# A gated graph network in groups of four tiles, with the next aggregation and s_hi moved ahead of z

## The chip, the cores and the metric

One core of one Trainium2 chip. The metric is the device time of an execution in microseconds (us). The kernel before has a median of 377.11 us over three runs (376.7 to 378.42).

## The reference, cut to what matters

Sixty-four graphs of 128 nodes with 128 features. A layer norm and a relu give the first state, five layers each aggregate over neighbours and update the state with a GRU cell, and the masked state is added to x.

```python
def _gru_cell(m, h, w_ih, w_hh, b_ih, b_hh):
    gi = m @ w_ih.T + b_ih
    gh = h @ w_hh.T + b_hh
    i_r, i_z, i_n = jnp.split(gi, 3, axis=-1)
    h_r, h_z, h_n = jnp.split(gh, 3, axis=-1)
    r = jax.nn.sigmoid(i_r + h_r)
    z = jax.nn.sigmoid(i_z + h_z)
    n = jnp.tanh(i_n + r * h_n)
    return (1.0 - z) * n + z * h
...
A = (adj != 0).astype(x.dtype)
h = jnp.maximum(_layernorm(x, axis=-1), 0.0)
for l in range(5):
    m = jnp.einsum('bnd,de->bne', h, weight[l])
    agg = jnp.einsum('bij,bid->bjd', A, m)
    h = _gru_cell(agg, h, w_ih, w_hh, b_ih, b_hh)
return x + h * mask[..., None]
```

## The kernel before, in words

**Tiles and units.** A tile is four graphs, so there are 16 tiles of 128 partitions x 512 columns. The state is kept with features on partitions (h, float32), with its fp16 high and low halves in hp. A unit is one layer of one tile, and there are 80 of them. `GROUPS = (4, 6, 6)` sets their order (line 45): layer 0 of all tiles of a group, then layer 1 of all, and so on. A tile's next layer thus comes four units later in the first group and six later in the others.

**One unit on TensorE** (lines 386 to 407). The layer's weight and w_ih are folded into one matrix V of that layer by `fold`, so that S, the aggregated state, is multiplied by V, and h by w_hh. Every float32 product is three fp16 matmuls (lines 273 to 275 for h, and for S). In order: the h products of r, z and n into ps_r, ps_z, ps_hn; the S products of r and z into the same banks; `aggregate(K + 1)`, eight small matmuls that sum over neighbours for the next unit into ps_s (lines 344 to 347); and the S product of n into ps_in. S products wait for s_lo of their unit, the h products of r, z and n for r, z and rhn of the unit before.

**The rest of a unit.** ScalarE (ACT): r = sigmoid(ps_r), z = sigmoid(ps_z), s_hi of the next unit (the fp16 part of ps_s), h_hi of the previous unit's state, and n = tanh. VectorE (DVE): rhn (ps_hn times r), the n input (ps_in + rhn), s_lo of the next unit, then (z - 1) times n and the new h. GpSimd (POOL): zh (z times h), then h_lo of the previous unit's state (line 783). Every engine works through its queue in the order that the code writes (`for K in range(N)` in each block), whatever is ready.

**The way back.** The aggregation needs the state with nodes on partitions. SyncE (SP) issues a DMA transpose nat<-hp (line 221) once h_lo is done, and `aggregate` waits for its landing (line 341).

**Preparing a tile** (`prep`, lines 53 to 61). While earlier tiles are in work, each tile from 4 on passes through nine stages, one per unit: 0 loads of adjacency and of an x, and moments on DVE; 1 their aggregate and minus_mean on DVE, 1/std on POOL; 2 the adjacency on POOL (line 766); 3 and 4 the two halves of the layer norm on ACT (line 417); 5 nat_hi on ACT and nat_lo on POOL; 6 the DMA transpose hp<-nat (line 209) and the float32 state. Tiles below `HALVES` (10) get that state from four float32 PE transposes (line 356) and a relu on ACT (line 437). Tiles from 10 on get it by splitting each float32 into two 16-bit halves on ACT (`split`, line 444), a DMA transpose of the halves (line 215), and a joining copy on DVE in stage 8 (`join`, line 648). Tiles are 3 units apart up to tile 9, and 5 apart after.

**Finishing a tile.** `ends` (line 60) says in which unit a tile's mask product (line 790) and its sum with x (line 794) run, both on POOL in one unit; SP stores the result an iteration later, and `load_ends` fetches x and the mask six units ahead. Unit 78 has its mask product on DVE.

**Folding.** `folding(K)` (line 187) puts the folds of layers 1 to 4 at the ends of units 2, 6, 10 and 14; ACT and DVE make v_hi and v_lo of them there.

Of the kernel before, what the change touches and what calls it, by code (L numbers as in the profile page):

```python
# [5 lines left out]
ALU = mybir.AluOpType  # L6
# [8 lines left out]
TG = 4  # L15
# [3 lines left out]
EPS = 1e-05  # L19
GROUPS = (4, 6, 6)  # L20
RING = 10
# [4 lines left out]
DIRECT = 1  # L26
HALVES = 10
FETCH = 6
FINISH = 5
STAGES = 9  # L30
EXPONENT = 0x7F800000
# [5 lines left out]
def gnn_kernel(nc, x, xT, adj, mask_row, fold_lhs, w_ihT, w_hhT, bias_ih, bias_hh, ident, out):  # L37
# [8 lines left out]
    N = len(units)  # L46
    at = {u: K for K, u in enumerate(units)}


# [4 lines left out]
    for t in reversed(range(FIRST, TILES)):  # L54
        gap = 3 if t < starts[1] + GROUPS[1] else 5
        prep[t] = min(at[t, 0] - STAGES, prep[t + 1] - gap if t + 1 < TILES else N)
    ends = {}
    for t in range(TILES - 1):
        soon = at[t, LAST] + 1
        ends[t] = soon if t >= starts[-1] or not t else max(soon, ends[t - 1] + 3)  # L60
    tile_at_stage = [{prep[t] + s: t for t in prep} for s in range(STAGES)]
    ending = {ends[t]: t for t in ends}
    fetching = {ends[t] - FETCH: [t] for t in ends}
    fetching[N - FINISH - FETCH].append(TILES - 1)

# [4 lines left out]
    with ExitStack() as ctx:  # L70
# [86 lines left out]
        nat_hi_init, nat_lo_init = sem("nat_hi_init"), sem("nat_lo_init")  # L157
        split_done = sem("split_done")
        h_hi_init, h_lo_init, h_init = sem("h_hi_init"), sem("h_lo_init"), sem("h_init")
# [34 lines left out]
        def _(sp):  # L194
# [16 lines left out]
            def transpose_halves(t):  # L211
                sp.wait_ge(split_done, t - HALVES + 1)
                if t - HALVES >= 2:
                    sp.wait_ge(h_init, t - 1)
                sp.dma_start_transpose(halves_t[:, t % 2], halves[:, t % 2].rearrange("p b c -> p (b c)")).then_inc(
                    halves_loaded[t % 2], 16)
# [35 lines left out]
            for K in range(1, N + 2):  # L252
# [6 lines left out]
                if K in tile_at_stage[6]:  # L259
                    transpose_first(tile_at_stage[6][K])  # L260
                    if tile_at_stage[6][K] >= HALVES:
                        transpose_halves(tile_at_stage[6][K])
                if K - 1 in ending:
                    store(ending[K - 1])
                for t in fetching.get(K, ()):
# [5 lines left out]
        def _(pe):  # L271
# [114 lines left out]
            for K in range(N):  # L386
                if K:
                    h_products(K)
                else:
                    first_h_products()  # L390
                if K == N - 1:
                    break
                pe.wait_ge(s_lo_done, K + 1)
                if K < L * FIRST and K % FIRST == 0:
                    pe.wait_ge(v_lo_done, units[K][1] + 1)
                s_product(K, 0, ps_r).then_inc(r_mm, 1)
                s_product(K, 1, ps_z).then_inc(z_mm, 1)
                if K + 1 < FIRST:
                    transpose_first(K + 1)
                if tile_at_stage[5].get(K, HALVES) < HALVES:  # L400
                    transpose_first(tile_at_stage[5][K])
                aggregate(K + 1)
                if K >= 2:
                    pe.wait_ge(h_done, K - 1)
                s_product(K, 2, ps_in[K % 2]).then_inc(in_mm, 1)
                if folding(K):
                    fold(folding(K))

        @block.scalar
        def _(act):  # L410
            def layernorm(t, half):
                act.wait_ge(shift_done, t + 1)
                if t >= LN:
                    act.wait_ge(nat_lo_init, t - LN + 1)
                    act.wait_ge(t_mm, min(t - LN + 1, HALVES))
                for q in (2 * half, 2 * half + 1):
# [14 lines left out]
            def transposed(t):  # L431
                act.wait_ge(t_mm, t + 1)
                if t < DIRECT:
                    act.wait_ge(h_lo_init, t + 1)
                if t >= RING:
                    act.wait_ge(masked, t - RING + 1)
                nc.scalar.activation(h[:, t % RING], ps_t[:], ACT.Relu).then_inc(h_init, 1)

            def split(t):

                act.wait_ge(h0_done, 2 * t + 2)
                if t - HALVES >= 2:
                    act.wait_ge(halves_loaded[t % 2], 16 * ((t - HALVES) // 2))
                nc.scalar.copy(halves[:, t % 2], h0[:, t % LN].bitcast(U16).rearrange("p (c b) -> p b c", b=2)).then_inc(
                    split_done, 1)
# [72 lines left out]
            for K in range(N):  # L518
                if K < N - 1:
# [3 lines left out]
                    if K == 1:  # L523
                        gate_n(0)
                    gate_z(K)
                    s_high(K + 1)
                else:
# [22 lines left out]
                if K in tile_at_stage[5]:  # L550
                    natural_high(tile_at_stage[5][K])
                if K in tile_at_stage[6] and tile_at_stage[6][K] < HALVES:
                    transposed(tile_at_stage[6][K])
                if K in tile_at_stage[6] and tile_at_stage[6][K] >= HALVES:
                    split(tile_at_stage[6][K])
# [3 lines left out]
        def _(dve):  # L559
# [47 lines left out]
            def new_state(K):  # L607
# [6 lines left out]
                dve.wait_ge(zn_done, K + 1)  # L614
                out_ap = h[:, t % RING] if K < N - 2 else ps_in[K % 2][:]
                nc.vector.tensor_tensor(out_ap, zh[:, K % 2], ps_in[K % 2][:], ALU.subtract).then_inc(h_done, 1)  # L616
# [26 lines left out]

            def join(t):
                dve.wait_ge(halves_loaded[t % 2], 16 * ((t - HALVES) // 2 + 1))
                if t >= RING:
                    dve.wait_ge(masked, t - RING + 1)
                nc.vector.tensor_copy(h[:, t % RING].bitcast(U16).rearrange("p (c b) -> p b c", b=2),
                               halves_t[:, t % 2].rearrange("p (b g) c -> p b (g c)", b=2)).then_inc(h_init, 1)

# [66 lines left out]
            for K in range(N):  # L717
# [10 lines left out]
                if K in tile_at_stage[1]:  # L728
                    aggregate(tile_at_stage[1][K])
                    opposite_mean(tile_at_stage[1][K])  # L730
                if tile_at_stage[8].get(K, 0) >= HALVES:
                    join(tile_at_stage[8][K])
                if K == 1:
# [3 lines left out]
                elif K:  # L737
                    masked_open(K)
                    last_result(K)
                if K == N - 2:  # L740
                    masked_state(K)
# [4 lines left out]
        def _(pool):  # L746
# [33 lines left out]
            def state_low(K):  # L780
                t = units[K][0]
                pool.wait_ge(h_hi_done, inner[K])
                nc.gpsimd.tensor_tensor(h_lo(t), h[:, t % RING], h_hi(t), ALU.subtract).then_inc(h_lo_done, 1)  # L783

            def final(t):
                f = t % FRING
                if t < TILES - 2:
                    pool.wait_ge(ends_loaded[f], 32 * (t // FRING + 1))
                    pool.wait_ge(h_done, at[t, LAST] + 1)
                    nc.gpsimd.tensor_tensor(mask_in[:, f], mask_in[:, f], h[:, t % RING], ALU.mult).then_inc(masked, 1)  # L790
                    pool.wait_ge(masked, t + 1)
                else:
                    pool.wait_ge(last_masked, 1)
                nc.gpsimd.tensor_tensor(x_out[:, f], x_out[:, f], mask_in[:, f], ALU.add).then_inc(out_done, 1)
# [27 lines left out]
            for K in range(N):  # L822
# [14 lines left out]
                if K == N - FINISH:  # L837
                    masked_last_h()
                if K in ending and K < N - 1:
                    final(ending[K])  # L840

# [35 lines left out]
```

## Time and profile before

| | before |
|---|---|
| median of 3 runs, us | 377.11 |
| the profiled execution, us | 377.65 |
| its span, first to last instruction, us | 375.9 |
| granted TensorE clock, share of full | 0.996 |
| busy share PE / DVE / ACT / POOL | 97 / 83 / 79 / 73 % |
| DMA queue q1, share of 16 engines' span | 51.7 % |

The span is one profiled execution; the time of the same execution is 1.75 us longer. A matmul's shown duration overlaps the next one's, so the start of one and the start of the next tell the pace, not the duration. In the prediction, a unit is counted from the start of its S product of r, "S of r" for short, and offsets are from there.

### The profile page before, as it was taken

How to read it: one execution, taken by the hardware profiler on the slowest of the kernel's cores; microseconds unless marked ns; L12 is line 12 of the kernel's file. 1: busy time of each engine (PE TensorE's matmuls, PEld its weight loads, DVE VectorE, ACT ScalarE, POOL GpSimd, SP SyncE). 2: the span in 40 equal slices, each digit the busy share in tenths (PEclk: the TensorE clock that was granted, in tenths of full speed). 3: DMA queues.
4: the chain of work that ended last, by engine and by line, in shares of the span. 5: the costliest groups of instructions: out<-in, count | busy, mean ns of one | idle time of the engine just before them, and what ended most of it. 6: DMA issues, size and time to landing. Idle time of an engine off the chain costs nothing.

```text
span 375.9 us, 6545 instructions
## 1 busy us (share of the span) xinstructions
PE 363.5 (97%) x2152; PEld 184.0 (49%) x2152; DVE 310.2 (83%) x572; ACT 297.6 (79%) x495; POOL 275.7 (73%) x258
## 2 busy tenths in 40 slices
PE   7899999999999999999999999999999999999992
PEld 3454555555555544445444545544455545555441
DVE  4879888888878788798989898888878787777775
ACT  5988898998878888798888887687677776677662
POOL 3759779788778979587695876867877655555796
PEclk9999999999999999999999999999999999999998
DMA  8536535747744556745364774327734423287422
GB/s 259 189 58 140 114 74 123 175 95 180 169 111 111 86 94 121 150 87 114 83 115 112 146 192 82 88 58 161 134 70 102 97 56 58 56 228 184 95 84 84
DMA packets 102176, 44.46 MB, mean 118 GB/s; under 512 B 91392, under 2 KB 91776, under 8 KB 102144
## 3 DMA queue, kind: packets, MB, share of 16 engines
q1 hardware_dynamic: 102000, 43.80, 51.7%
q8 instruction: 17, 0.28, 0.3%
q10 hardware_dynamic: 144, 0.26, 0.2%
q14 instruction: 15, 0.12, 0.1%
HBM read 17.57 MB, written 4.19 MB: 58 GB/s over the span
## 4 chain that ended last, share of the span: by engine, by line
PE 79%; DVE 9%; POOL 5%; DMA 2%; issue 2%; SPq 1%; ACT 1%; DVEq 0%; POOLq 0%
PE ps_r L273 8%; PE ps_z L275 8%; PE ps_z L274 8%; PE ps_z L273 8%; PE ps_r L275 8%; PE ps_r L274 8%; PE ps_s L347 4%; PE ps_s L346 4%; PE ps_in L275 4%; PE ps_in L274 4%; PE ps_in L273 4%; PE ps_hn L273 4%; PE ps_hn L275 4%; PE ps_hn L274 4%; DVE ps_in L605 1%
## 5 line engine op out<-in xcount | busy, mean ns | idle before, releaser
L778 POOL TENSOR_TENSOR zh<-z,h 128x512 f32<-128x512 f32 x80 | 101.8, 1272 | 77.3 <-ACT z L461 77.0
L455 ACT ACTIVATE r<-ps_r,b_sum,unscale 128x512 f32<-128x512 f32 x80 | 62.2, 778 | 46.9 <-PE ps_r L275 46.0
L465 ACT ACTIVATE ps_in<-ps_in,b_ih,unscale 128x512 f32<-128x512 f32 x80 | 60.0, 751 | 19.2 <-DVE ps_in L605 17.5
L783 POOL TENSOR_TENSOR hp<-h,hp 128x512 f16<-128x512 f32 x64 | 74.0, 1156 | 1.3 <-ACT hp L471 1.3
L599 DVE SCALAR_TENSOR_TENSOR rhn<-ps_hn,b_hn,r 128x512 f32<-128x512 f32 x80 | 59.9, 749 | 17.1 <-ACT r L455 16.8
L605 DVE TENSOR_TENSOR ps_in<-ps_in,rhn 128x512 f32<-128x512 f32 x80 | 56.0, 699 | 16.0 <-PE ps_in L275 13.7
L611 DVE SCALAR_TENSOR_TENSOR ps_in<-z,ps_in 128x512 f32<-128x512 f32 x79 | 54.6, 691 | 11.0 <-ACT ps_in L465 11.0
L461 ACT ACTIVATE z<-ps_z,b_sum,unscale 128x512 f32<-128x512 f32 x80 | 61.6, 770 | 0.7 <-PE ps_z L275 0.7
L616 DVE TENSOR_TENSOR h<-zh,ps_in 128x512 f32<-128x512 f32 x78 | 53.6, 687 | 10.3 <-POOL zh L778 2.1
L593 DVE TENSOR_TENSOR s_lo<-ps_s,s_hi 128x512 f16<-128x512 f32 x80 | 54.4, 680 | 0.4 <-ACT s_hi L449 0.4
L449 ACT CAST s_hi<-ps_s 128x512 f16<-128x512 f32 x80 | 46.6, 582 | 0.5
L346 PE MATMUL ps_s<-a,nat 128*128 128x128 f16 x320 | 44.3, 219 | 0.0
L347 PE MATMUL ps_s<-a,nat 128*128 128x128 f16 x320 | 44.3, 219 | 0.0
L471 ACT CAST hp<-h 128x512 f16<-128x512 f32 x64 | 40.6, 634 | 2.1 <-DVE h L616 2.1
L346 PEld LDWEIGHTS ps_s<-a,nat 128*128 128x128 f16 x320 | 31.3, 98 | 8.8 <-POOL nat L760 0.4
L347 PEld LDWEIGHTS ps_s<-a,nat 128*128 128x128 f16 x320 | 31.3, 98 | 8.2
L273 PE MATMUL ps_r<-s_hi,v_hi 128*128 128x512 f16 x80 | 30.4, 380 | 2.8 <-DVE s_lo L593 2.6
L273 PE MATMUL ps_z<-s_hi,v_hi 128*128 128x512 f16 x80 | 30.3, 379 | 0.0
L274 PE MATMUL ps_r<-s_lo,v_hi 128*128 128x512 f16 x80 | 30.3, 379 | 0.0
L275 PE MATMUL ps_r<-s_hi,v_lo 128*128 128x512 f16 x80 | 30.3, 379 | 0.0
L274 PE MATMUL ps_z<-s_lo,v_hi 128*128 128x512 f16 x80 | 30.3, 379 | 0.0
L275 PE MATMUL ps_z<-s_hi,v_lo 128*128 128x512 f16 x80 | 30.3, 379 | 0.0
(109 smaller groups left out, 741.3 us busy)
## 6 DMA issues: line engine op xcount, KB each, us to landing
x_in<-in_x SPq DMA_DIRECT2D x16, 256.0 KB, 3.7
adj_in<-in_adj SPq DMA_DIRECT2D x16, 256.0 KB, 3.9
x_out<-in_xT SPq DMA_DIRECT2D x16, 256.0 KB, 3.1
mask_in<-in_mask_row SPq DMA_DIRECT2D x16, 256.0 KB, 3.6
out<-x_out SPq DMA_DIRECT2D x15, 256.0 KB, 2.3
nat<-hp SPq DMA_TRANSPOSE x64, 3.1
fold_in<-in_fold_lhs SPq DMA_DIRECT2D x1, 320.0 KB, 3.9
out<-x_out ACTq DMA_DIRECT2D x1, 256.0 KB, 2.6
```

The source lines that it names most:

```text
L273: nc.tensor.matmul(ps[:], w_hi, m_hi, start=start, stop=False)
L274: nc.tensor.matmul(ps[:], w_hi, m_lo, start=False, stop=False)
L275: return nc.tensor.matmul(ps[:], w_lo, m_hi, start=False, stop=stop)
L346: nc.tensor.matmul(block_of(ps_s, q), block_of(nat_hi(t), q), a_q, start=True, stop=False)
L347: last = nc.tensor.matmul(block_of(ps_s, q), block_of(nat_lo(t), q), a_q, start=False, stop=True)
L455: nc.scalar.activation(r[:], ps_r[:], ACT.Sigmoid, bias=b_sum[:, 0:1], scale=unscale[:, 0:1]).then_inc(r_done, 1)
L461: nc.scalar.activation(z[:, K % 2], ps_z[:], ACT.Sigmoid, bias=b_sum[:, 1:2], scale=unscale[:, 0:1]).then_inc(z_done, 1)
L465: nc.scalar.activation(ps_in[K % 2][:], ps_in[K % 2][:], ACT.Tanh, bias=b_ih[:, 2:3], scale=unscale[:, 0:1]).then_inc(n_done, 1)
L599: nc.vector.scalar_tensor_tensor(out=rhn[:], in0=ps_hn[:], scalar=b_hn[:, 0:1], in1=r[:], op0=ALU.add, op1=ALU.mult).then_inc(rhn_done, 1)
L605: nc.vector.tensor_tensor(ps_in[K % 2][:], ps_in[K % 2][:], rhn[:], ALU.add).then_inc(npre_done, 1)
L778: nc.gpsimd.tensor_tensor(zh[:, K % 2], z[:, K % 2], h[:, t % RING], ALU.mult).then_inc(zh_done, 1)
L783: nc.gpsimd.tensor_tensor(h_lo(t), h[:, t % RING], h_hi(t), ALU.subtract).then_inc(h_lo_done, 1)
```

## The change

`GROUPS` becomes (4, 4, 4, 4). All tiles from 4 on take the way over split, DMA transpose and join. The join is cut in two, in stages 8 and 9, so a preparation has ten stages. With the new constants the tiles 4 to 8 start their preparation at units 4, 7, 10, 13 and 18, tile 9 at 23, and the others every five units from there to 53. The mask product and the final sum of a finished tile run in consecutive units on POOL (units 21 and 22 for tile 0, then every five units up to tile 7 at 56 and 57, then every three); the last group's mask products, units 76 to 78, run on DVE, and its states go to PSUM. Layer 1 is folded in unit 0, ahead of TensorE's wait for s_lo. TensorE does the next aggregation between the S products of r and z, and ACT does s_hi of the next unit ahead of z.

```diff
--- before.py
+++ after.py
@@ -17,17 +17,17 @@
-GROUPS = (4, 6, 6)
+GROUPS = (4, 4, 4, 4)
...
-HALVES = 10
 FETCH = 6
-FINISH = 5
-STAGES = 9
+FINISH = 3
+STAGES = 10
+SPREAD = 5
@@ -45,6 +45,7 @@
+    END = at[starts[-1], LAST]
@@ -52,16 +53,27 @@
     for t in reversed(range(FIRST, TILES)):
-        gap = 3 if t < starts[1] + GROUPS[1] else 5
+        gap = 3 if t < starts[1] + GROUPS[1] else SPREAD
         prep[t] = min(at[t, 0] - STAGES, prep[t + 1] - gap if t + 1 < TILES else N)
     ends = {}
     for t in range(TILES - 1):
         soon = at[t, LAST] + 1
-        ends[t] = soon if t >= starts[-1] or not t else max(soon, ends[t - 1] + 3)
+        if t >= starts[-1]:
+            ends[t] = soon
+        elif t and ends[t - 1] > prep[TILES - 1]:
+            ends[t] = max(soon, ends[t - 1] + 3)
+        else:
+            ends[t] = max(soon, ends[t - 1] + SPREAD if t else 0)
+            ends[t] += (prep[TILES - 1] + 3 - ends[t]) % SPREAD
...
+    adds = {t: ends[t] + (ends[t] + 1 not in ending and ends[t] + 2 < N) for t in ends}
+    adding = {adds[t]: t for t in ends if t < TILES - 2}
+    storing = {adds[t] + 1: t for t in ends}
@@ -258,10 +270,9 @@
                 if K in tile_at_stage[6]:
                     transpose_first(tile_at_stage[6][K])
-                    if tile_at_stage[6][K] >= HALVES:
-                        transpose_halves(tile_at_stage[6][K])
-                if K - 1 in ending:
-                    store(ending[K - 1])
+                    transpose_halves(tile_at_stage[6][K])
+                if K in storing:
+                    store(storing[K])
@@ -390,20 +401,20 @@
                 if K == N - 1:
                     break
+                if K == 0:
+                    fold(1)
                 pe.wait_ge(s_lo_done, K + 1)
                 if K < L * FIRST and K % FIRST == 0:
                     pe.wait_ge(v_lo_done, units[K][1] + 1)
                 s_product(K, 0, ps_r).then_inc(r_mm, 1)
-                s_product(K, 1, ps_z).then_inc(z_mm, 1)
                 if K + 1 < FIRST:
                     transpose_first(K + 1)
-                if tile_at_stage[5].get(K, HALVES) < HALVES:
-                    transpose_first(tile_at_stage[5][K])
                 aggregate(K + 1)
+                s_product(K, 1, ps_z).then_inc(z_mm, 1)
                 if K >= 2:
                     pe.wait_ge(h_done, K - 1)
                 s_product(K, 2, ps_in[K % 2]).then_inc(in_mm, 1)
-                if folding(K):
+                if folding(K) > 1:
                     fold(folding(K))
@@ -522,8 +531,8 @@
+                    s_high(K + 1)
                     gate_z(K)
-                    s_high(K + 1)
@@ -549,9 +558,7 @@
-                if K in tile_at_stage[6] and tile_at_stage[6][K] < HALVES:
-                    transposed(tile_at_stage[6][K])
-                if K in tile_at_stage[6] and tile_at_stage[6][K] >= HALVES:
+                if K in tile_at_stage[6]:
                     split(tile_at_stage[6][K])
@@ -612,7 +619,7 @@
-                out_ap = h[:, t % RING] if K < N - 2 else ps_in[K % 2][:]
+                out_ap = h[:, t % RING] if K < END else ps_in[K % 2][:]
@@ -641,12 +648,17 @@
-            def join(t):
-                dve.wait_ge(halves_loaded[t % 2], 16 * ((t - HALVES) // 2 + 1))
+            def join(t, half):
+
+                dve.wait_ge(halves_loaded[t % 2], 16 * ((t - FIRST) // 2 + 1))
                 if t >= RING:
                     dve.wait_ge(masked, t - RING + 1)
-                nc.vector.tensor_copy(h[:, t % RING].bitcast(U16).rearrange("p (c b) -> p b c", b=2),
-                               halves_t[:, t % 2].rearrange("p (b g) c -> p b (g c)", b=2)).then_inc(h_init, 1)
+                two = slice(2 * half, 2 * half + 2)
+                state = h[:, t % RING].rearrange("p (g c) -> p g c", g=TG)[:, two].rearrange("p g c -> p (g c)")
+                joined = nc.vector.tensor_copy(state.bitcast(U16).rearrange("p (c b) -> p b c", b=2),
+                                               halves_t[:, t % 2].rearrange("p (b g) c -> p b g c", b=2)[:, :, two].rearrange(
+                                                   "p b g c -> p b (g c)"))
+                joined.then_inc(h_init if half else half_joined, 1)
@@ -728,8 +740,9 @@
-                if tile_at_stage[8].get(K, 0) >= HALVES:
-                    join(tile_at_stage[8][K])
+                for half in range(2):
+                    if K in tile_at_stage[8 + half]:
+                        join(tile_at_stage[8 + half][K], half)
@@ -737,7 +750,7 @@
-                if K == N - 2:
+                if END <= K < N - 1:
                     masked_state(K)
@@ -782,15 +795,18 @@
+            def masked_result(t):
+                f = t % FRING
+                pool.wait_ge(ends_loaded[f], 32 * (t // FRING + 1))
+                pool.wait_ge(h_done, at[t, LAST] + 1)
+                nc.gpsimd.tensor_tensor(mask_in[:, f], mask_in[:, f], h[:, t % RING], ALU.mult).then_inc(masked, 1)
+
             def final(t):
                 f = t % FRING
-                if t < TILES - 2:
-                    pool.wait_ge(ends_loaded[f], 32 * (t // FRING + 1))
-                    pool.wait_ge(h_done, at[t, LAST] + 1)
-                    nc.gpsimd.tensor_tensor(mask_in[:, f], mask_in[:, f], h[:, t % RING], ALU.mult).then_inc(masked, 1)
+                if t < starts[-1]:
                     pool.wait_ge(masked, t + 1)
                 else:
-                    pool.wait_ge(last_masked, 1)
+                    pool.wait_ge(last_masked, t - starts[-1] + 1)
                 nc.gpsimd.tensor_tensor(x_out[:, f], x_out[:, f], mask_in[:, f], ALU.add).then_inc(out_done, 1)
@@ -836,8 +852,10 @@
-                if K in ending and K < N - 1:
-                    final(ending[K])
+                if K in ending and ending[K] < starts[-1]:
+                    masked_result(ending[K])
+                if K in adding:
+                    final(adding[K])
```

## Rows read from the trace of the kernel before

**Rows 1.** Section 1 of the page: busy us, share of the span, instructions.
```profile
PE 363.5 (97%) x2152; PEld 184.0 (49%) x2152; DVE 310.2 (83%) x572; ACT 297.6 (79%) x495; POOL 275.7 (73%) x258
```
**Rows 2.** Timeline of unit 64: start us, us, engine, line, operation, [idle before it].
```profile
301.86 0.38 PE L273 MATMUL ps_r<-s_hi,v_hi 128*128 128x512 f16 x1
...
302.71 0.78 ACT L455 ACTIVATE r<-ps_r,b_sum,unscale 128x512 f32<-128x512 f32 x1 [1.11 <-PE ps_r L275]
...
303.39 0.77 ACT L461 ACTIVATE z<-ps_z,b_sum,unscale 128x512 f32<-128x512 f32 x1
303.52 0.75 DVE L599 SCALAR_TENSOR_TENSOR rhn<-ps_hn,b_hn,r 128x512 f32<-128x512 f32 x1 [0.40 <-ACT r L455]
...
304.05 0.58 ACT L449 CAST s_hi<-ps_s 128x512 f16<-128x512 f32 x1
304.23 1.27 POOL L778 TENSOR_TENSOR zh<-z,h 128x512 f32<-128x512 f32 x1 [1.95 <-ACT z L461]
...
304.45 0.70 DVE L605 TENSOR_TENSOR ps_in<-ps_in,rhn 128x512 f32<-128x512 f32 x1 [0.18 <-PE ps_in L275]
...
304.51 0.64 ACT L471 CAST hp<-h 128x512 f16<-128x512 f32 x1
...
304.90 0.38 PE L273 MATMUL ps_z<-hp,u_hi 128*128 128x512 f16 x1
305.06 0.68 DVE L593 TENSOR_TENSOR s_lo<-ps_s,s_hi 128x512 f16<-128x512 f32 x1
...
305.97 0.69 DVE L611 SCALAR_TENSOR_TENSOR ps_in<-z,ps_in 128x512 f32<-128x512 f32 x1 [0.23 <-ACT ps_in L465]
...
306.19 0.38 PE L273 MATMUL ps_r<-s_hi,v_hi 128*128 128x512 f16 x1
```
**Rows 3.** Windows view of units 4 to 77: busy us of each engine, clock, DMA.
```profile
34.00:362.50 328.50, 326.69 (x1954) 166.44 (x1955) 276.92 (x479) 264.95 (x433) 245.32 (x219) 1.00 0.53 114
```
**Rows 4.** The chain that ended last, between 34 and 363 us: start us, us, what.
```profile
44.13 0.44 PE ps_t L356 x4
45.66 0.65 PE ps_f L362 x2
...
113.22 0.44 PE ps_t L356 x4
```
**Rows 5.** Groups of instructions: busy us, mean ns of one | idle before.
```profile
L417 ACT ACTIVATE h<-x_in,shift,rstd 128x128 f32<-128x128 f32 x64 | 27.4, 484 | 0.0
L766 POOL TENSOR_SCALAR a<-adj_in 128x512 f16<-128x512 f32 x12 | 23.2, 1935 | 0.0
...
L444 ACT COPY halves<-h 128x1024 uint16<-128x1024 uint16 x6 | 6.2, 1033 | 0.0
```
**Rows 6.** Timeline of units 1 to 3: DVE, the queue of SP, TensorE's weight loads.
```profile
23.23 0.86 DVE L565 BATCH_NORM_STATS2 bn<-x_in 128x6 f32<-128x128 f32 x4
...
27.40 1.23 SPq L221 DMA_TRANSPOSE nat<-hp  x1
...
30.50 0.10 PEld L346 LDWEIGHTS ps_s<-a,nat 128*128 128x128 f16 x1 [0.26 <-DMA nat<-hp]
```
**Rows 7.** Landings: line 221 of the whole run, then the one issued at 121.3.
```profile
DMA to landing us min/median/max: 3.0/3.1/4.8
...
nat<-hp SPq DMA_TRANSPOSE x1, 4.5
```
**Rows 8.** Timeline of POOL and DVE in units 39 and 54.
```profile
196.11 1.16 POOL L783 TENSOR_TENSOR hp<-h,hp 128x512 f16<-128x512 f32 x1
196.31 1.57 DVE L648 COPY h<-halves_t 128x1024 uint16<-128x1024 uint16 x1
...
263.07 1.74 POOL L790 TENSOR_TENSOR mask_in<-mask_in,h 128x512 f32<-128x512 f32 x1
```
**Rows 9.** Timeline of POOL and DVE in unit 37.
```profile
187.45 1.16 POOL L783 TENSOR_TENSOR hp<-h,hp 128x512 f16<-128x512 f32 x1
...
188.04 0.58 DVE L579 TENSOR_SCALAR minus_mean<-mean_var 128x4 f32<-128x4 f32 x1
```

More of the change, by code:

```diff
@@ L59, in gnn_kernel @@
         soon = at[t, LAST] + 1
-        ends[t] = soon if t >= starts[-1] or not t else max(soon, ends[t - 1] + 3)
+        if t >= starts[-1]:
[5 more added lines that the diff above has]
+            ends[t] += (prep[TILES - 1] + 3 - ends[t]) % SPREAD
     tile_at_stage = [{prep[t] + s: t for t in prep} for s in range(STAGES)]
     ending = {ends[t]: t for t in ends}
+    adds = {t: ends[t] + (ends[t] + 1 not in ending and ends[t] + 2 < N) for t in ends}
+    adding = {adds[t]: t for t in ends if t < TILES - 2}
+    storing = {adds[t] + 1: t for t in ends}
     fetching = {ends[t] - FETCH: [t] for t in ends}
-    fetching[N - FINISH - FETCH].append(TILES - 1)
+    fetching.setdefault(N - FINISH - FETCH, []).append(TILES - 1)
     xT_t = xT.rearrange("d (t c) -> t d c", c=TILE)
@@ L157, in gnn_kernel @@
         nat_hi_init, nat_lo_init = sem("nat_hi_init"), sem("nat_lo_init")
-        split_done = sem("split_done")
+        split_done, half_joined = sem("split_done"), sem("half_joined")
         h_hi_init, h_lo_init, h_init = sem("h_hi_init"), sem("h_lo_init"), sem("h_init")
@@ L211, in transpose_halves @@
             def transpose_halves(t):
-                sp.wait_ge(split_done, t - HALVES + 1)
-                if t - HALVES >= 2:
+                sp.wait_ge(split_done, t - FIRST + 1)
+                if t - FIRST >= 2:
                     sp.wait_ge(h_init, t - 1)
@@ L414, in layernorm @@
                     act.wait_ge(nat_lo_init, t - LN + 1)
-                    act.wait_ge(t_mm, min(t - LN + 1, HALVES))
+                    act.wait_ge(t_mm, min(t - LN + 1, FIRST))
                 for q in (2 * half, 2 * half + 1):
@@ L434, in transposed @@
                     act.wait_ge(h_lo_init, t + 1)
-                if t >= RING:
-                    act.wait_ge(masked, t - RING + 1)
                 nc.scalar.activation(h[:, t % RING], ps_t[:], ACT.Relu).then_inc(h_init, 1)
@@ L441, in split @@
                 act.wait_ge(h0_done, 2 * t + 2)
-                if t - HALVES >= 2:
-                    act.wait_ge(halves_loaded[t % 2], 16 * ((t - HALVES) // 2))
+                if t - FIRST >= 2:
+                    act.wait_ge(halves_loaded[t % 2], 16 * ((t - FIRST) // 2))
                 nc.scalar.copy(halves[:, t % 2], h0[:, t % LN].bitcast(U16).rearrange("p (c b) -> p b c", b=2)).then_inc(
```

## Prediction

> **What bounds the kernel now.** I read the page first, then the timeline of one undisturbed unit, then the chain for what interrupts such units. TensorE is busy for 363.5 of 375.9 us [rows 1], so only two things can shorten the run: fewer TensorE instructions, or fewer pauses. The timeline of unit 64 [rows 2] gives the unit: S of r starts at 301.86, that of the next unit at 306.19, so 4.33 us. In it the other engines are ready by these amounts (offsets from 301.86): ACT sits idle 1.11 before r (0.85), then does r, z (1.53) and s_hi (2.19); DVE idles 0.40 before rhn, 0.18 before the n input (2.59) and 0.23 before 1-z times n (4.11), 0.81 in all; its s_lo is done at 3.88, 0.45 ahead of S; POOL idles 1.95 before z times h (2.37 to 3.64), then does h_lo, 1.16 long [rows 8], to 4.76.
>
> From unit 4's S (34.00) to unit 78's (362.50) are 328.50 us [rows 3]. 74 units of 4.33 make 320.4. The chain [rows 4] shows what else is there: six groups of PE transposes (tiles 4 to 9, first at 44.13, last at 113.22) of 0.44, so 2.6; three foldings (layers 2 to 4) of 0.65, so 1.95. The remainder, 328.5 - 320.4 - 2.6 - 1.95 = 3.5, is S waiting for s_lo, mostly one or two units after a join or after POOL had an adjacency and a finished tile together.
>
> **What goes.** Tiles 4 to 9 take the split, DMA transpose and join of the later tiles: -2.6. Joins come in halves in two units, POOL's work of a finished tile in two units, one POOL job per unit from tile 9 on: the longest, the adjacency at 1.94 [rows 5], just fits the 1.95 idle. The old stalls go: -3.5. DVE gets two masked states more at the end, as long as its other products (0.69 in [rows 2]), under its 0.81: 0.
>
> **First units.** Folding 1 moves into TensorE's wait for s_lo of unit 0: -0.65 on TensorE. But unit 3's aggregation needs the first transposed state. It began at 30.50, just as that landed (issued 27.40, and 3.05 on) [rows 6]. The new order asks for it 0.65 + 0.65 earlier, at 29.3 instead of 30.6. Tile 4's moments (0.86 at 23.23) leave DVE there, so the state comes some 0.75 earlier, 29.7, and 0.4 is still waited. The gain is between 0 (no earlier state) and 0.9 (no wait); I take 0.4.
>
> **The reordering.** S of r, aggregation, S of z, S of n. The aggregation comes 0.65 earlier (three matmuls of 0.22). It brings s_lo nothing in a plain unit: DVE does s_lo after the n input, which waits for S of n, unmoved. ACT now does s_hi first, so z starts at 1.53 + 0.47 (s_hi's step in [rows 2], from 304.05 to the h_hi cast behind it) = 2.00, 0.47 later, and ends at 2.77. The next h product of z starts at 3.04: margin 0.2, so 0 where ACT is on time. POOL starts 0.47 later too: z times h 2.84 to 4.11, before DVE's need at 4.80; h_lo ends at 5.23.
>
> **Groups of four.** Now the state must be back in three units instead of five. h_lo ends at 5.23 of the next unit, the transpose lands 3.1 later [rows 7], at 8.3; the aggregation wants it at 2 x 4.33 + 0.65 = 9.3. Margin 1.0, 0.8 if the weight load counts; before, with the aggregation 0.65 later and z 0.47 earlier, it was 2.1 in group 1 and two units more in the groups of six. Landings lie between 3.0 and 4.8 [rows 7], so each of some 60 costs 0 to 0.8. Late ones: 4.5, behind adjacency, x and store issued together [rows 7], a bunch which now comes for tiles 9 to 11, at 0.5 for every second: 0.8; the longest, 4.8, came behind four loads, which recur at unit 71: 0.8; and two more with nothing in the order of issues to explain them, at 0.5 as the 4.5: 1.0. Together 2.6, bounds 0 and 6.
>
> **The shared port.** A join that starts while POOL runs an instruction ends 0.60 behind that one's end: 196.31 + 1.57 = 197.88 against 196.11 + 1.16 = 197.27; and a mask product on POOL that began at 263.07, beside a later join, took 1.74 instead of 1.27 [rows 8]. So each engine holds the other off for a whole instruction. The half join should be near 0.35 behind POOL's end. It is issued at 3.80 and z times h ends at 4.11: it ends at 4.46, inside DVE's 0.81, if it gets in before h_lo; h_lo is 0.35 later for it. The little minus_mean likewise took 0.58 and ended with h_lo [rows 9]. It now ends at 5.25, 1.14 late, less 0.40 and 0.18 is 0.56 against 0.45: 0.1 in six units, 0.6. Bounds 0 (it ends with z times h) and 1.2 (twice that).
> The Trainium skill, "SBUF — State Buffer", section "SBUF: two separate sides", says that VectorE in a two-port mode and GpSimd take an exclusive lock, whoever starts first, and the other is blocked; the rows agree for joins. If h_lo counts as the one that starts first at the end of z times h, the rule gives the rival "lost port" below, 383 us; if the waiting join does, it gives the sum.
>
> **Early tiles, three units apart.** Tiles 4 to 8 now also carry split and join. ACT: half a layernorm is 0.86 (27.4 us in 32 halves) and the split 1.03 [rows 5]; both fall in units 10, 13 and 16: 1.89 - 1.11 = 0.78 late, of which unit 10 gets some back from folding. Against z's margin of 0.2 that costs 0.35 to 0.55: 1.1 for three. DVE: moments 0.86 [rows 6] and half a join (0.66) in unit 18, aggregate and half a join in 19: backlog 0.71, then 1.2 more less 0.81, against 0.45: 0.6. Transposes: SP issues nat, adjacency, x, hp and halves, three of them transposes of 1.23 [rows 6], in a unit of 4.33, and POOL's adjacency with nat_lo (3.1 against 1.95) delays h_lo: next landings 0.65 and 0.6 beyond the margin, of which the ACT pauses hide over half: 0.5. Together 2.2, bounds 0.5 and 5 (nothing overlaps, next group's joins too).
>
> **Last unit.** Unit 79 begins with the h products of z, not of r, so z of 78, now 0.47 later, has no 0.65 of r products ahead of it. Between 0 and 0.47 is lost; S then waits for s_lo anyway: +0.2.
>
> **Sum**, against the profiled execution: -2.6 - 3.5 - 0.4 + 2.6 + 0.6 + 2.2 + 0.2 = -0.9, span 375.0. That execution took 377.65 for a span of 375.9, and the runs' median is 377.11. Taken off the median: 376.2 us.
>
> **Rivals.**
> *Margins hold* (faster). Most transposes land in 3.1 and the 1.0 covers them; only ACT's and DVE's early pauses stay (1.7): -2.6 - 3.5 - 0.4 + 0.2 + 1.7 = -4.6, 372.5. For it: the median landing is 3.1, and a pause anywhere gives the transposes behind it as much slack. Against: the 4.5 needed no more than the three transfers that come together again. Chance 0.22.
> *Lost port* (slower). If POOL's h_lo, already queued when z times h ends, gets the port before the waiting half join, the join ends at 5.25 + 0.35 = 5.6; DVE is 1.49 late, less 0.58 is 0.91 against 0.45: 0.45 in each of some 20 units with a half join and an h_lo: +9, less 2 that cover late landings: 383. It decides if more than about six half joins end behind h_lo. Against it stands the 1.74 row. Chance 0.10.
> *Late states* (slower). The aggregation becomes the regular wait: if a landing is over 4.1 in two of every five units, 25 x 0.3 = 7.5 in place of 2.6: 381. For it: 12 tiles now send halves through the same queue, formerly 6. Chance 0.14.
> *No earlier S.* That s_hi ahead of z helps nothing is in my sum already.
>
> **How the numbers follow.** 0.5% (1.9 us, about what a measurement can tell) is 375.2 to 379.0. My case, with the three added terms (5.4) between 3 and 7.7 instead, spans 373.8 to 378.5 and has 0.54: 0.14 of it below 375.2, 0.40 within the band. Faster is then 0.22 + 0.14 = 0.36, same 0.40, slower 0.10 + 0.14 = 0.24. The range, 372.6 to 380.5, leaves out the lost port, some of the late states and a little below margins hold.
>
> **What would show it.** In the changed profile: no ps_t group after tile 3; z starting 2.0 after S of r in plain units and h_lo ending at 5.2; PE's waits no longer for s_lo but before ps_s for nat, in a handful of units, with landings over 4; pauses before ps_z's h product in units 11, 14 and 17; half joins of 0.6 that end 0.35 behind z times h. If half joins take 1.7, the port is lost. If ps_s waits in over 15 units, states are late. If units 24 to 70 run at 4.33 throughout, I have overpriced the margin. A plain unit above 4.33 would prove the z margin wrong: 0.1 over 60 units is 6 us.

## The result and the profile after

The changed kernel takes 382.29 us (median of 6 runs, 381.21 to 382.97) against 377.1 for the kernel before on the same chip (376.64 to 378.42). The ratio is 1.013, with a 95% interval of 1.0107 to 1.0153: slower by 1.3%, where the prediction said 376.2 and a range of 372.6 to 380.5. The profiled execution has a span of 380.7 us, 4.8 more than before.

From the page of the changed kernel: section 1, then from section 3 the main queue and the queue that carries instructions, then landings (section 6).

```profile
span 380.7 us, 6533 instructions
...
PE 363.8 (96%) x2128; PEld 179.9 (47%) x2128; DVE 320.0 (84%) x592; ACT 302.9 (80%) x495; POOL 277.1 (73%) x256
...
q1 hardware_dynamic: 108336, 45.37, 53.6%
q8 instruction: 17, 0.28, 0.3%
...
nat<-hp SPq DMA_TRANSPOSE x64, 3.1
```

TensorE has 24 instructions fewer than in [rows 1], the PE transposes of tiles 4 to 9, and still the run is longer. The 4.8 us are pauses, and the view of waits says before what. Columns: engine and line that waited, what for, us in total, times, longest.

```profile
PEld ps_s L357 <- DMA nat<-hp: 13.2, 15, 1.3
...
PE ps_s L357 <- DMA nat<-hp: 6.3, 11, 0.8
PEld ps_r L284 <- DVE s_lo L600: 6.0, 14, 0.8
...
PEld ps_z L284 <- ACT z L470: 2.4, 5, 0.7
```

Before, the first of these was 0.3 us, once; the wait of S for s_lo was 7.9 in 11. So the regular wait has moved from s_lo to the aggregation's wait for the transposed state. (The weight load runs ahead of its matmul, so of a wait of 1.3 only 0.7 to 0.9 is lost.)

The windows view from unit 4's S to unit 78's, which answers to [rows 3] and has its columns, and its first part, up to unit 19:

```profile
34.01:367.61 333.60, 326.44 (x1931) 162.16 (x1930) 287.40 (x507) 269.99 (x432) 250.03 (x221) 1.00 0.55 119
34.01:104.00 69.99, 68.20 (x395) 32.89 (x394) 62.94 (x118) 58.89 (x98) 51.11 (x48) 1.00 0.58 120
```

333.6 less 74 x 4.33 and 1.95 of folding leaves 11.2 of pauses, where the kernel before had 3.5 and 2.6 of PE transposes. Counted unit by unit, from the start of one S of r to the next, 3.6 lie in units 6 to 17, where the early tiles are prepared, and 7.5 behind unit 22: nine units with 0.36 to 0.94 and four with 0.11 or 0.12. Units with nothing extra in them take 4.33, as before.

One of the nine, from the chain that ended last: start us, us, what.

```profile
313.33 0.22 PE ps_r L284
...
314.01 0.47 ACT r L464
...
314.69 0.58 ACT s_hi L458
315.27 0.69 ACT z L470
...
316.02 0.49 POOL zh L791
...
317.25 1.17 POOL hp L796
318.44 4.81 DMA nat<-hp
323.30 0.23 PE ps_s L357
```

The chain begins with r of one unit and goes through the reordered s_hi and z to zh, to h_lo of the unit before, to a transpose that takes 4.81 instead of 3.1, and TensorE waits at its end. The timeline there shows the loss (0.66 on the matmul) and what else stood idle:

```profile
323.29 0.10 PEld L357 LDWEIGHTS ps_s<-a,nat 128*128 128x128 f16 x1 [1.15 <-DMA nat<-hp]
323.30 0.23 PE L357 MATMUL ps_s<-a,nat 128*128 128x128 f16 x1 [0.66 <-DMA nat<-hp]
```

**Why that landing was late.** The DMA view of the transpose issued at 318.44, between 318 and 323 us, then of the last 2.2 us before 323.4, then of 322.1 to 322.3 alone, and of a punctual one issued at 314.11, between 313.5 and 318 (each GB/s figure is a fortieth of its window):

```profile
GB/s 0 0 0 0 0 0 0 0 0 66 0 0 10 137 215 219 209 162 125 186 211 207 260 101 33 154 0 0 0 0 0 0 0 0 0 0 0 0 0 0
...
q1 hardware_dynamic: 1056, 0.26, 30.6%
q8 instruction: 1, 0.02, 1.2%
```
```profile
DMA packets 7, 0.02 MB, mean 8 GB/s; under 512 B 6, under 2 KB 6, under 8 KB 6
...
q8 instruction: 1, 0.02, 2.6%
q1 hardware_dynamic: 6, 0.00, 0.3%
```
```profile
q1 hardware_dynamic: 2, 0.00, 1.4%
```
```profile
GB/s 0 0 0 0 0 0 0 0 0 0 0 0 0 0 0 9 139 218 230 221 205 212 216 198 221 177 214 67 5 0 0 0 0 0 0 0 0 0 0 0
...
q1 hardware_dynamic: 1056, 0.26, 30.7%
```

In both, the 1056 packets of the transpose start some 1.2 us behind the issue. In the punctual one they are all through 1.4 us later, at 2.6 behind the issue, and it lands at 3.1. In the late one all but two are through by 321.2, 2.8 behind the issue (the last figure, 154, is mostly the instruction packet). Then comes one packet of 16 KB on the instruction queue q8, from 321.24 to 322.17, and the transpose's last two packets, of 4 bytes each, start only at 322.15 and 322.16. The landing follows at 318.44 + 4.81 = 323.25. Of the other four late transposes with nothing beside them but such a packet, those issued at 62.4 and 359.2 look the same, with two packets left; those at 210.8 and 250.7, where the 16 KB packet comes 2.2 behind the issue, have 25 and 24 packets that start only when it ends.

There are 17 such packets in the run, one each 21 us or so, for 4256 instructions of TensorE and its weight loads. Eleven of the 64 landings take 4.3 us or more (4 before). Ten of them have one of these packets 2.1 to 2.9 behind their issue (packets and issues matched by their start times); only one, 4.45 at 264.4, has none, and it was issued right behind an adjacency load, a store, and loads of x and the mask.

### The profile page after: what moved, and what is told of

It is laid out like the page before. It is cut to its first block, busy times and chain, and to the rows that moved or that the text cites. A ratio compares the mean times of both kernels' runs of the same rounds, so it can differ in the third digit from the quotient of the medians.

```text
span 380.7 us, 6533 instructions
## 1 busy us (share of the span) xinstructions
PE 363.8 (96%) x2128; PEld 179.9 (47%) x2128; DVE 320.0 (84%) x592; ACT 302.9 (80%) x495; POOL 277.1 (73%) x256
## 4 chain that ended last, share of the span: by engine, by line
PE 59%; DMA 16%; ACT 8%; POOL 7%; issue 5%; DVE 3%; SPq 1%; DVEq 0%; POOLq 0%; ACTq 0%
DMA nat<-hp 12%; PE ps_z L284 6%; PE ps_r L284 6%; PE ps_z L286 6%; PE ps_z L285 6%; PE ps_r L286 6%; PE ps_r L285 6%; POOL hp L796 4%; PE ps_s L357 3%; PE ps_s L358 3%; PE ps_in L286 3%; PE ps_hn L286 3%; PE ps_in L285 3%; PE ps_hn L285 3%; PE ps_hn L284 3%
## 5 line engine op out<-in xcount | busy, mean ns | idle before, releaser
L796 POOL TENSOR_TENSOR hp<-h,hp 128x512 f16<-128x512 f32 x64 | 77.3, 1207 | 0.0
L470 ACT ACTIVATE z<-ps_z,b_sum,unscale 128x512 f32<-128x512 f32 x80 | 63.2, 790 | 1.5 <-PE ps_z L286 0.7
L623 DVE TENSOR_TENSOR h<-zh,ps_in 128x512 f32<-128x512 f32 x76 | 52.3, 688 | 8.3 <-DVE ps_in L618 0.5
L480 ACT CAST hp<-h 128x512 f16<-128x512 f32 x64 | 39.7, 621 | 0.6 <-DVE h L623 0.6
L284 PE MATMUL ps_z<-hp,u_hi 128*128 128x512 f16 x79 | 30.0, 380 | 0.7 <-ACT z L470 0.6
L284 PE MATMUL ps_r<-hp,u_hi 128*128 128x512 f16 x79 | 30.0, 379 | 0.7 <-DMA hp<-nat 0.7
```

Of the source, the lines that this page charges most:

```text
L284: nc.tensor.matmul(ps[:], w_hi, m_hi, start=start, stop=False)
L470: nc.scalar.activation(z[:, K % 2], ps_z[:], ACT.Sigmoid, bias=b_sum[:, 1:2], scale=unscale[:, 0:1]).then_inc(z_done, 1)
```

## The experiments

**The theory** after the result (A): the two reorderings take from the state's way back what groups of four need. Aggregation comes 0.65 earlier and z, zh and h_lo 0.47 later, so the margin before the aggregation, 1.9 with the older orders, is 0.75, and landings that are 1.4 to 1.8 late pass it. The rest of the change is a gain. Rivals: groups of four alone are too short for the landings (B); the crowd of preparation and half joins is at fault (C); only one of the two orders does it (D); the late landings come from where TensorE's instruction stream happens to stand (E). Times are medians, ratios against the kernel before on the same chip. Landings of 4.3 us or more ("late") are counted of 64, each kernel in its one profiled execution, and "pauses" means units 4 to 77, as above.

### Both orders as before

```diff
                 s_product(K, 0, ps_r).then_inc(r_mm, 1)
+                s_product(K, 1, ps_z).then_inc(z_mm, 1)
...
                 aggregate(K + 1)
-                s_product(K, 1, ps_z).then_inc(z_mm, 1)
...
-                    s_high(K + 1)
                     gate_z(K)
+                    s_high(K + 1)
```

> The changed kernel with the old order back on TensorE (aggregation behind S of z) and on ACT (z ahead of s_hi). Theory A (thin margin: in groups of four the state lands only 0.6 to 0.9 us before the early aggregation asks for it, and every landing of 4.5 to 4.9 stalls TensorE): the margin grows by 1.12 to about 1.9 and covers those landings, pauses before ps_s fall from 13 us of weight-load waits to under 3, time near 374 (372.5 to 376). Theory B (the groups of four and the crowded preparation cost the time, whatever the order): 381 to 383.

Measured: 374.06 us, ratio 0.9902 (0.9887 to 0.9916), span 371.6. Pauses fall from 11.2 to 1.7. The same waits:

```profile
PEld ps_r L284 <- DVE s_lo L600: 8.5, 28, 0.6
...
PEld ps_s L357 <- DMA nat<-hp: 0.9, 2, 0.7
```

So in groups of four the reordering costs 8.2 us, and the rest of the change is a gain of 1.0%; this kernel beats both. B and C fall as causes by themselves: the groups, the crowd and the half joins are all still here. What was not expected: only one landing is over 4.3. The older order did not just bear late landings, it had hardly any. And yet eleven of its transposes have an instruction packet 2.4 to 3.0 behind their issue, and these land at 3.04 to 3.45. So a packet beside a transpose is not enough to make it late.

### One order at a time

First ACT's order as before, TensorE's as changed.

```diff
-                    s_high(K + 1)
                     gate_z(K)
+                    s_high(K + 1)
```

> The changed kernel with z ahead of s_hi again on ACT, TensorE's new order kept. z cannot start before its product, which is done 1.94 behind S of r, and it started at 2.00. Theory A: within 0.5 us of the changed kernel, 382; s_hi is later and still ready before the n input. Theory C (it is s_hi ahead of z that delays z, h_lo and the landing): most of the gain of both orders back, 376 or less.

Measured: 382.75 us, ratio 1.0139 (1.0117 to 1.0161), 12 late landings, pauses 11.4: the same as the changed kernel. Whether s_hi or z comes first on ACT is of no weight once S of z stands behind the aggregation, since z then waits for its product (it starts 1.94 behind S of r instead of 2.00).

Then TensorE's order as before, ACT's as changed.

```diff
                 s_product(K, 0, ps_r).then_inc(r_mm, 1)
+                s_product(K, 1, ps_z).then_inc(z_mm, 1)
...
                 aggregate(K + 1)
-                s_product(K, 1, ps_z).then_inc(z_mm, 1)
```

> The changed kernel with the aggregation behind S of z again, s_hi kept ahead of z. s_hi now waits for the later aggregation (1.95), z starts at 2.4 and ends at 3.2, against 3.04 at which the h product of z would start. Theory A with the z margin of 0.2 as read: each plain unit takes 4.5 instead of 4.33, so 12 to 15 us more, less what late landings no longer cost: 388 to 396. Theory B: 382. If the z margin is larger than read: 378.

Measured: 391.86 us, ratio 1.0374 (1.0357 to 1.0391). Here s_hi waits for the later aggregation and z for s_hi, so every plain unit is 0.24 longer:

```profile
PEld ps_z L284 <- ACT z L470: 41.0, 74, 0.8
```

So the margin of 0.2 between z's end and the h product of z, read from [rows 2], is real, and what passes it is paid in each unit. D: TensorE's order alone is enough; ACT's alone is worse. It too makes landings late, eight of them, each with an instruction packet 1.9 to 2.9 behind its issue, though TensorE's order is the older one: z is later, and so the transposes of plain units go out 1.13 behind S of r, where they went out at 0.46 with both orders as before and at 0.95 in the changed kernel.

### The reordering in the kernel before

Groups of 4, 6 and 6 and everything else as before, with the two reorderings (the first diff the other way round).

> The kernel before (groups 4, 6, 6) with the two reorderings alone. Theory A: only the first group of four has a thin margin, two or three landings there cost 0.5 to 0.9 each; 378 to 380. If the reordering costs in every unit: 382 or more.

Measured: 380.75 us, ratio 1.0079 (1.0061 to 1.0097), a little above the span of what was expected; 1.0 of it is lost before unit 4 and 0.3 at the end. The telling number is another: 12 landings over 4.3, where the kernel before has 4, yet `ps_s` waits only 2.0 us, 4 times. The reordering makes landings late in these groups too. All four waits are in units 3 to 13; the nine late landings behind them, in the groups of six, make TensorE wait for none.

### The state's cast and h_lo earlier

h_hi right behind r on ACT, and h_lo ahead of zh on POOL, so that the transpose goes out earlier whatever z does.

```diff
                     gate_r(K)
+                    if K > 1 and units[K - 1][1] < LAST:
+                        state_high(K - 1)
...
+                if K > 1 and units[K - 1][1] < LAST:
+                    state_low(K - 1)
                 kept(K)
```

On the changed kernel:

> The changed kernel, both reorderings kept, but h_hi of the previous unit's state is made on ACT right behind r, and POOL does h_lo in its idle time ahead of z times h instead of behind it. The transpose is issued near 3.4 behind S of r instead of 5.25, so the margin of the early aggregation grows from 0.75 to about 2.6. Theory A (margin): the pauses before ps_s are gone although the order is new; z is some 0.17 later, just inside its 0.2; 373 to 376. Theory D (the new order costs the time in some other way than through the state's return): 380 or more. If z's margin is overrun by 0.05: 379.

Measured: 395.16 us, ratio 1.0465 (1.0446 to 1.0484), a miss. `ps_s` waits for nat once, 0.5 us, so the pauses of the state are gone, as meant; but z now stands behind two casts, h_hi and s_hi, which the expectation had overlooked:

```profile
PEld ps_z L284 <- ACT z L470: 43.7, 63, 1.2
```

With z ahead of s_hi and TensorE's order as before:

> The same early h_hi and h_lo with the old order on TensorE and ACT. Theory A: the kernel with the old orders has only 1.7 us of pauses left, all for s_lo, so there is little to win from margin: within 1 us of it, 373.5 to 374.5. z then ends at 2.93, inside its margin. Theory D has no reason for a change either; a gain of over 1 us would say that late states still cost there.

Measured: 384.45 us, ratio 1.0174 (1.0154 to 1.0194), a miss too. Plain units take 4.33, but in every unit with a tile's work on DVE the h of the unit before is late, and ACT, which works through its queue in order, waits for it with z and s_hi behind:

```profile
PEld ps_z L284 <- ACT z L470: 27.7, 61, 1.1
ACT hp L480 <- DVE h L623: 14.5, 36, 0.8
DVE s_lo L600 <- ACT s_hi L458: 13.6, 35, 1.0
```

The same with TensorE's changed order, to see what the aggregation's place is worth when the state has time:

> The early h_hi and h_lo with the new order on TensorE and the old one on ACT (r, h_hi, z, s_hi), which is the run with old orders and early state (384.45) but for TensorE's order. Theory A: with the state early the place of the aggregation costs nothing: 383.5 to 385.5, no pauses before ps_s for nat beyond 1 us. If the early aggregation costs something else too: 388 or more.

Measured: 384.57 us (2 runs), ratio 1.0176 (1.0127 to 1.0224), 0.1 from its sister, and unit by unit the same pauses. With an early state, the aggregation's place costs nothing and brings nothing. That fits A's second half, that it costs only through the state; but both kernels are 10 us slower than with both orders as before and wait for z 60 times, so a small cost of another kind could be hidden there.

### Whole joins

```diff
             def join(t, half):
+                if half == 0:
+                    return
...
+                nc.vector.tensor_copy(h[:, t % RING].bitcast(U16).rearrange("p (c b) -> p b c", b=2),
+                               halves_t[:, t % 2].rearrange("p (b g) c -> p b (g c)", b=2)).then_inc(h_init, 1)
```

This is put on the kernel with both orders as before; the whole join stands where the second half stood.

> The kernel with the old orders and the join done whole, in the later of its two units. From the shared port: it is issued beside h_lo, ends 0.60 behind it, s_lo comes 0.68 late against a margin of 0.45: 0.2 in each of nine late tiles and more in the crowded units 13 to 19; 2 to 3 us more than with halves. If halving is worth nothing: within 0.5.

Measured: 374.98 us, ratio 0.9929 (0.9909 to 0.995), 0.9 above halves, less than expected. The intervals of the two ratios overlap a little, but the trace has the loss in its place: 0.2 to 0.3 in each of nine units with a later join, nothing more among the early tiles. The halving is a small part of the gain.

### Instruction packets elsewhere

The changed kernel with its first warm-up as 64 matmuls of 128 columns instead of 16 of 512. That is 48 matmuls and 48 weight loads more, so every later instruction of TensorE lies 96 further on in its stream.

```diff
-                awake(16)
+                awake(64, P)
```

> The changed kernel with the 16 first idle matmuls of 512 columns replaced by 64 of 128 columns: the same stretch of time, 96 instructions more on TensorE ahead of all work. Theory A with the instruction queue as the cause of late landings: still every nat landing of 4.3 us or more has a 16 KB packet of the instruction queue between issue and landing, some 8 to 12 of them, but in other units than 8, 22, 41, 50; time 381 to 384. If late landings come from the kernel's own loads and stores, they stay in the same units.

Measured: 384.99 us (2 runs), ratio 1.0193 (1.0162 to 1.0223). The time is above what was expected (381 to 384): one landing took 5.8 us, the longest of all runs, and cost a pause of 1.7. Again 10 landings are over 4.3, nine of them with an instruction packet 1.9 to 2.8 behind their issue, and but for one in other units than in the changed kernel. The packets have a say in which landings are late, as E has it, but this other placing did not lower their number.

### Groups of 4, 6 and 6

The changed kernel, and then the one with both orders as before, with the groups of the kernel before (`GROUPS = (4, 6, 6)`, preparation from unit 1 on, tiles finished by the older rule).

> The changed kernel, both reorderings and the split of all tiles kept, with the groups 4, 6 and 6 of before (first preparation at unit 1, tiles finished as before but in two units). From unit 20 on the state then has two units more. Theory A: the pauses before ps_s for nat vanish from unit 24 on (7 to 8 us of them), landings of 4.5 to 4.9 go on as often as in the changed kernel but cost nothing; six tiles instead of five are now prepared three units apart, which costs 1 to 2 more: 375 to 378. Theory B (groups of four are not what makes the order costly): 381 or more.

Measured: 380.15 us, ratio 1.0071 (1.0049 to 1.0093), above the expectation. There are still 10 late landings, but behind unit 22 no pause is left over 0.4 (two, of 0.37 and 0.24): groups of six have the room. The first units and the crowded preparation (5.8 us in units 5 to 19) were dearer than thought.

> The same groups with the old orders on TensorE and ACT. Theory A: z has its margin again in the crowded units and the first group its state; 1.5 to 3 us below the reordered one, 373.5 to 375.5, and no better than groups of four with the old orders (374.1). A clearly lower time would say that groups of four cost something by themselves.

Measured: 376.06 us, ratio 0.9951 (0.9934 to 0.9968), a little above, with three late landings. With the older orders, groups of four are better by 2.0 us, most of it in units 5 to 19, where they have pauses of 1.3 instead of 3.1.

### Only the moment of issue

What was open: why the older order has 1 late landing and the changed one 11. Groups of four and both orders as before; only POOL clears a scratch, 0.46 us long, ahead of each h_lo, from unit 22 on. In plain units the transpose then goes out 0.86 behind S of r instead of 0.46.

```diff
                 pool.wait_ge(h_hi_done, inner[K])
+                if K >= 22:
+                    nc.gpsimd.memset(pad[:, K % 2], 0.0)
```

> Both orders as before, groups of four; only, from unit 22 on, POOL clears a scratch of 128x440 (about 0.47 us, from 0.10 for 4 and 0.20 for 128 columns) ahead of each h_lo, so that h_lo ends at about 5.23 and the state's transpose is issued at about 5.25 of the next unit, as in the changed kernel, while z, s_hi and TensorE's order stay where they were. Theory P (it is the moment of the issue against TensorE's instruction packets that makes landings late, not the order of the matmuls): 7 to 9 of the landings behind unit 22 are over 4.3 us, each with an instruction packet 2.1 to 2.9 us behind its issue, though with the older order there was one. The margin falls from 1.92 to 1.45, so each costs only about 0.2 to 0.3: 375 to 376.5 us, about 1.5 above the both-back kernel's 374.06. Theory O (the aggregation's place in TensorE's stream moves the packets; POOL's 0.47 does not matter): 0 to 2 such landings and 374.0 to 374.5 us. If POOL's extra 0.47 delays anything else (POOL idles 1.3 in a plain unit, less beside a finished tile's work), units with a mask product or an adjacency show it, before ps_s only through longer waits for nat.

Measured: 374.71 us, ratio 0.9918 (0.9897 to 0.9938), span 372.9; pauses 2.9 instead of 1.7. The pad, the landings of the transposes (from their line), and who waited:

```profile
L798 POOL MEMSET pad<- 128x440 f32 x46 | 21.3, 463 | 0.0
```
```profile
  PEld ps_s L358: 4.5, 10
  PE ps_s L358: 0.4, 2
...
DMA to landing us min/median/max: 3.0/3.1/4.8
```

Eight landings behind unit 22 are over 4.3, where the same kernel without the pad has one, and seven of them have an instruction packet 2.0 to 2.8 behind their issue (an eighth packet so placed did no harm). The count is as theory P had it, that the moment of the issue does it. The cost, 0.65 us by the medians, is below what I gave it, since most fell where 1.45 of margin was nearly enough; the two ratios' intervals overlap, so the count and the pauses carry this, and not the time. Neither TensorE's order nor ACT's is needed for late landings, then: a later issue alone makes them.

All eleven kernels with h_lo behind zh say the same. Their traces hold 112 transposes with an instruction packet 1.8 to 3.1 behind the issue. Of the 42 issued up to 0.65 behind S of r, two are late; of the 70 issued at 0.82 or more, 67 are.

Why 0.4 us decides is open. The packets come later in the unit too: mostly 2.7 to 3.5 behind S of r with both orders as before, 3.3 to 3.8 in the changed kernel. Their distance behind the issue is nearly the same, 2.4 to 3.0 and 2.1 to 2.9. With both orders as before, where nothing else was in the queue, the transpose's packets had all started 2.6 behind the issue, before or within 0.2 of the instruction packet's start; ten of the eleven landings stayed at 3.04 to 3.15, and eight of the packets took 1.2 to 1.6 us. In the five late ones of the changed kernel shown above the last packets of the transpose start only when the instruction packet ends; it takes 0.9 to 1.1, and the landing comes 1.4 to 1.8 later. What puts the instruction packet ahead of them no run here shows.

## Why the prediction was wrong

- **What goes**: right. The PE transposes left (2.6, no ps_t group behind tile 3), and so did the old stalls (3.5).
- **First units**: right, -0.4. Counted from unit 0's S, unit 4 comes 0.37 sooner; in this one execution the start was 0.38 later and hid it.
- **The reordering in a plain unit**: right to within 0.02. z starts 2.00 behind S of r and ends at 2.78, zh runs 2.86 to 4.13, h_lo ends at 5.25, the transpose lands at 8.35; the weight load wanted it at 9.10. A margin of 0.75; I had 0.8 with the weight load counted. The unit stayed 4.33, and s_lo gained nothing.
- **The shared port**: right, and it leaves no room for "lost port". The half join gets in behind zh, ahead of h_lo; and minus_mean takes 1.08 and ends with h_lo, at 0.11 in each of four units where I had 0.1 in six:

```profile
298.92 0.65 DVE L658 COPY h<-halves_t 128x512 uint16<-128x512 uint16 x1
...
299.21 1.34 POOL L796 TENSOR_TENSOR hp<-h,hp 128x512 f16<-128x512 f32 x1
```
```profile
152.83 1.16 POOL L796 TENSOR_TENSOR hp<-h,hp 128x512 f16<-128x512 f32 x1
...
152.94 1.08 DVE L586 TENSOR_SCALAR minus_mean<-mean_var 128x4 f32<-128x4 f32 x1
```

- **Early tiles**: the right kind, too small. 3.6 instead of 2.2, 0.8 of the difference one late landing at unit 6. ACT's pauses before the h product of z stand in units 11, 14 and 17, as said, and in 15. With both orders as before the same tiles cost 1.3, so most of this, too, is the reordering's.
- **Last unit**: the step is right, unit 78 is 0.28 longer where I had +0.2. But from unit 78's S to the end took 13.1 instead of 13.35, so -0.25 in all, since the last store landed 2.1 behind its issue and not 2.6, a thing not in my sum.
- **Late landings: the step that failed.** "Together 2.6, bounds 0 and 6": it took four or five landings out of the kernel before, explained two of them by bunches of loads, and priced them at 0.5 to 0.8 each. Measured: nine pauses, one for each late landing, and 6.9 us behind unit 22, and the one of 0.8 at unit 6. Two things in it were wrong. The cause: page section 3 of the kernel before lists the instruction queue, and I had read past it; three of its four landings over 4.3 have such a packet 1.9 to 2.7 behind their issue (as have eight punctual ones, up to 3.0 behind). The fourth, the 4.83 behind four loads, has none, so for that one my explanation may stand. And the rate: I carried it over as if it were a property of the transfers, while the reordering moved the issue from 0.46 to 0.95 behind S of r, and late landings are 11 of 64 instead of 4 (12 with the reordering alone, in the groups of before). Each then costs mostly 0.7 to 0.9, about what a landing of 4.5 to 4.9 leaves when 3.1 and the margin of 0.75 are taken off. The margin I had right; how many landings would pass it I had not.

Of the rivals, "late states" (381, chance 0.14) came nearest. Its test was that ps_s waits in over 15 units: the weight loads wait 15 times, the matmuls 11, so it stands just at the line. Its number is near by luck. It had 25 landings over 4.1 at 0.3 each, where ten cost mostly 0.7 to 0.9; and its reason, more halves through the same queue, was wrong: with both orders as before the same halves went through that queue, and one landing was late. "Margins hold" (372.5) has its like in the kernel with both orders as before, 374.1. In sum, 375.9 - 2.6 - 3.5 + 3.6 + 7.5 - 0.25 = 380.65, against 380.7 (the first units' 0.4 and the later start cancel). The 7.5 holds 0.5 of minus_mean's.

## What to carry to other kernels

A result that has to come back within a round has a margin, and the margin must be held against the worst landing (4.9 in the changed kernel, 5.8 in one of its variants), not the median (3.1). Read the margin in the timeline before an edit that shifts both of its ends, and don't take the share of late landings from the kernel before: here it went by when the transfer is issued. A reordering that frees nothing on the path that sets the pace (here S waits for s_lo, and s_lo for the n input) has only margins to spend; put it in alone and time it alone.

## What was not expected of the hardware

- **Transfers land late beside instruction packets.** Ten of the eleven landings of 4.3 us and more in the changed kernel (the median is 3.1) have beside them one 16 KB packet of 0.9 to 1.1 us on the instruction queue q8, whose packets keep step with TensorE's stream; no wait of TensorE's matmuls in this trace falls to them. The Trainium skill, "Runtime: NRT & Kernel Launch", section "Instruction fetch mechanics", says that an engine's sequencer fetches its instructions in blocks of 16 KiB, 256 instructions, over a DMA queue of its own, and that the cost is "mostly hidden". Size and number agree (17 packets, 0.28 MB, for 4256 instructions); hidden it is for the engine, but not for who waits on another queue.
- **Less than half a microsecond decides.** Late landings behind unit 22 are one or eight, by whether the transposes of plain units go out 0.46 or 0.86 behind S of r (374.06 and 374.71 us), and where nothing else is beside them, the late ones' last packets start only when the instruction packet is through.
- **Joins and the port.** A half join takes 0.65 behind zh in the changed kernel and 0.70 on average; with both orders as before h_lo has begun when it is issued (3.60 against 3.79 behind S of r), so the first halves take 1.28 and the mean is 1.03, and it is still hidden. A small DVE instruction of 128x4, 0.17 by itself, takes 1.08 when it starts 0.1 behind POOL's h_lo.
